# Four graph-attention layers on one core: the unmasked attention computed transposed, its denominators from column sums, and three kinds of elementwise work moved to ScalarE

## The reference

```python
out = relu(x @ mlp1_w + mlp1_b)                  # 512 features
residual = out
h = relu(out) @ W_fc                             # 512 x 512
e = leaky_relu(f1[:, None] + f2[None, :], 0.2)   # f1, f2: h times the halves of a_fc
att = softmax(e, axis=2)                         # over j, no mask
out = elu(elu(att @ h)) + residual
out = relu(out @ mlp2_w + mlp2_b)                # 256 features
...                                              # masked attention with W_hand, elu(elu(.)) + residual, relu
```

## Time and profile before

| quantity | value |
|---|---|
| median of 3 runs | 2882.01 us (2877.89 to 2885.95) |
| the profiled execution, its own time | 2880.97 us |
| span of its trace | 2879.2 us |
| mean granted TensorE clock | 0.996 of full speed |
| PE busy | 2827.2 us (98%) |
| DVE busy | 2551.1 us (89%) |
| ACT busy | 2169.4 us (75%) |
| POOL busy | 575.6 us (20%) |
| DMA over the span | 13 GB/s |

### The profile page before, as it was taken

The page is one execution under the profiler, slowest core; times in us unless marked ns, Lnnn a source line. Parts: engine busy times, 40 slices in busy tenths (PEclk is TensorE's granted clock), DMA queues, the critical chain, the costliest instruction groups (busy, mean ns, idle before and its releaser), DMA issues. The chain is left out here.

```text
span 2879.2 us, 66889 instructions
## 1 busy us (share of the span) xinstructions
PE 2827.2 (98%) x25368; PEld 2593.7 (90%) x25368; DVE 2551.1 (89%) x7305; ACT 2169.4 (75%) x5791; POOL 575.6 (20%) x731
## 2 busy tenths in 40 slices
PE   7999999999999999999999999999999999999998
PEld 7888998999999999998999999999989998999986
DVE  6898888998999899989988989889899888998977
ACT  5677778777777777787777787777777777777766
POOL 4021022211122211122211222111222111222001
PEclk8999999999999999999999999999999999999999
DMA  2000000000000000000000000000000000000000
GB/s 82 9 10 8 16 16 16 1 16 16 16 16 16 1 16 16 16 16 9 9 16 16 16 16 9 9 16 16 16 16 2 16 16 16 16 16 2 9 8 15
DMA packets 16800, 42.05 MB, mean 15 GB/s; under 512 B 5344, under 2 KB 7392, under 8 KB 16480
## 3 DMA queue, kind: packets, MB, share of 16 engines
q1 hardware_dynamic: 16480, 37.77, 3.7%
HBM read 20.99 MB, written 16.78 MB: 13 GB/s over the span
## 5 line engine op out<-in xcount | busy, mean ns | idle before, releaser
L690 PE MATMUL bank<-hw,R 128*128 128x257 f32 x3072 | 716.5, 381 | 4.4 <-DVE R L905 2.0
L690 PEld LDWEIGHTS bank<-hw,R 128*128 128x128 f32 x3072 | 562.2, 190 | 85.7 <-issue 11.1
L1380 POOL TENSOR_TENSOR rs<-ve,mhalf 128x4 f32<-128x4 f32 x128 | 133.5, 1043 | 1754.7 <-DVE ve L848 1649.5
L905 DVE SCALAR_TENSOR_TENSOR R<-bank,E,mask_ne 128x512 f32<-128x512 f32 x640 | 451.0, 741 | 19.1 <-PE bank L678 16.3
L592 PE MATMUL bank<-wfc_hi,oThi 128*128 128x256 f32 (+1 forms) x1024 | 302.5, 295 | 0.0
L592 PE MATMUL bank<-wfc_hi,oTlo 128*128 128x256 f32 (+1 forms) x1024 | 289.6, 283 | 0.0
L592 PE MATMUL bank<-wfc_lo,oThi 128*128 128x256 f32 (+1 forms) x1024 | 289.6, 283 | 0.0
L724 PEld LDWEIGHTS bank<-hw,R 128*64 128x64 f32 x8192 | 252.2, 139 | 29.3 <-issue 16.7
L724 PE MATMUL bank<-hw,R 128*64 128x65 f32 x8192 | 270.5, 225 | 6.6 <-DVE R L905 4.1
L1197 ACT ACTIVATE Z<-bank,rs 128x258 f32<-128x258 f32 (+1 forms) x384 | 177.8, 477 | 81.1 <-PE bank L592 80.8
L592 PEld LDWEIGHTS bank<-wfc_hi,oThi 128*128 128x128 f32 x1024 | 194.0, 189 | 1.7
(11 more groups left out here) (275 smaller groups left out, 8807.5 us busy)
## 6 DMA issues: line engine op xcount, KB each, us to landing
x<-in_x_dram SPq DMA_DIRECT2D x32, 512.0 KB, 3.5
out_dram<-x SPq DMA_DIRECT2D x31, 512.0 KB, 2.6
R<-in_adj_dram SPq DMA_DIRECT2D x2, 512.0 KB, 7.1
Z<-in_L_gnn_mlp_w_dram SPq DMA_DIRECT2D x2, 512.0 KB, 5.5
O<-in_L_gnn_W_fc_dram SPq DMA_DIRECT2D x1, 1024.0 KB, 6.8
out_dram<-x SPq DMA_DIRECT2D x4, 128.0 KB, 1.7
R<-in_L_gnn_W_dram SPq DMA_DIRECT2D x1, 256.0 KB, 3.8
R<-in_L_gnn_W_hand_dram SPq DMA_DIRECT2D x1, 256.0 KB, 6.6
```

Source lines behind the costliest of these rows:

```text
L690: ins = e.matmul(bk[:, 0:257], P[:, j, i * 128:(i + 1) * 128], hw[:, j, 0:257], start=(j == 0), stop=(j == NBLK - 1))
L905: e.scalar_tensor_tensor(P[:, t, :], bank_of(b, "row", p)[:, :], m["E"][:, 1, h, j:j + 1], mask[:, j, :], ALU.max, ALU.mult).then_inc(up(" ...
L1380: e.tensor_tensor(m["rs" + z][:, :], m["ve" + z][:, :], mhalf[:, :], ALU.pow).then_inc(up("rs", b), 1 if l == 1 else 3)
```

## The change

- **Inner attention.** Features are now the weights and P is streamed, 512 wide: four units `u` of 12 matmuls. The result is features x nodes at once, so the transposes `zT` are gone. `HA` loses its two extra columns.
- **Denominators.** POOL adds the four P blocks (`column_sums`: three additions of 128x512, a copy to hi, a subtraction for lo). PE sums over the partitions with 8 matmuls that stream two columns of ones, DVE takes the four reciprocals, PE spreads them over the partitions with 4 transposes, and ACT copies the row to `R[s][:, 3, :]`. DVE multiplies each unit by it (`scaled`).
- **The double elu.** ACT works on 512-wide tiles: relu of the negative, exp of its negative, second exp. DVE adds the residual to the relu part (`residual`) and joins (`joined`). The hi part goes to `Rr`, the lo part to `Zr`, so `oT` is free after `attf`, and ACT's next `m1` waits for `attf` of the batch before and no longer for its `m2`.
- **The order around P.** P is built before most of the lo parts of `HB`, and `USES` differs for lane 2.
- **Moved to ScalarE.** `center` of layers 2 and 3, and the minimum in layer 1's second attention (as relu of the negative and exp of its negative).
- `TURNS` is another table: `-        "w00ww0000ww0ww0000w00w11w0www0ww1111www1www00ww00w01...` becomes `+        "w00ww0000ww0ww0000ww0w011w0111101ww11wwwwwwww1001ww0...`, for every engine.

```diff
-        HA = {p: sb(f"HA{p}", [128, NBLK, F + 2], F32R) for p in PARTS2}
+        HA = {p: sb(f"HA{p}", [128, NBLK, F], F32R) for p in PARTS2}
...
-                    e.tensor_scalar(m["mn"][:, n:n + 1], m["sx"][:, n:n + 1], 1.0 / F, None, ALU.mult).then_inc(up("hn", b))
+                    e.activation(m["mn"][:, n:n + 1], m["sx"][:, n:n + 1], ACT.Copy, scale=-1.0 / F).then_inc(up("hn", b))
                     w.wait_ge(*at("hn", b, l - 2, n, 0))
-                    e.tensor_scalar(hns[s][:, n, :], x[:, n, :], m["mn"][:, n:n + 1], 0.0, ALU.subtract, ALU.max).then_inc(up("hn", b))
+                    e.activation(hns[s][:, n, :], x[:, n, :], ACT.Relu, bias=m["mn"][:, n:n + 1]).then_inc(up("hn", b))
...
-            for q in range(8):
-                i, H, n = q // 2, (HA, HB[s])[q % 2], 258 - q % 2 * 2
-                cols = slice(i * 128, (i + 1) * 128)
-                w.wait_ge(*freed(b, "attf", q))
+            def denominators():
+                w.wait_ge(*at("pq", b, 4))
+                w.wait_ge(*freed(b, "dn"))
+                bk = bank_of(b, "dn")
+                for i in range(NBLK):
+                    for k, c0 in enumerate((1536 + i * 128, i * 128)):
+                        ins = e.matmul(bk[:, 2 * i:2 * i + 2], Zr[s][:, c0:c0 + 128], ones[:, 0:2], start=k == 0, stop=k == 1)
+                ins.then_inc(up("dn", b))
+                yield
+                w.wait_ge(*at("rDf", b, 0))
+                for n in range(NBLK):
+                    ins = e.transpose(bk[:, n * 128:(n + 1) * 128], m["rD"][:, 0, n:n + 1].broadcast_to([128, 128]), ident[:, :])
+                ins.then_inc(up("dn", b))
+                yield
+
+            if len(RINGS[s]) == 2:
+                yield from denominators()
+            for u in range(4):
+                H, cols = (HA, HB[s])[u // 2], slice(u % 2 * 128, (u % 2 + 1) * 128)
+                w.wait_ge(*freed(b, "attf", u))
                 for j in range(NBLK):
                     w.wait_ge(*at("Plo", b, j))
-                    w.wait_ge(*at(("hAlo", "hBlo")[q % 2], b, j))
-                    ins = mm3(e, bank_of(b, "attf", q)[:, 0:n], (oT["hi"][:, j, cols], oT["lo"][:, j, cols]),
-                              (H["hi"][:, j, 0:n], H["lo"][:, j, 0:n]), j == 0, j == NBLK - 1)
-                    if j < NBLK - 1 and not i:
+                    w.wait_ge(*at(("hAlo", "hBlo")[u // 2], b, j))
+                    ins = mm3(e, bank_of(b, "attf", u)[:, :], (H["hi"][:, j, cols], H["lo"][:, j, cols]),
+                              (oT["hi"][:, j, :], oT["lo"][:, j, :]), j == 0, j == NBLK - 1)
+                    if j < NBLK - 1:
                         yield
                 ins.then_inc(up("attf", b))
                 yield
-            for fo in range(4):
-                w.wait_ge(*freed(b, "zT", fo))
-                bk = bank_of(b, "zT", fo)
-                c0 = (fo * 128 + 256) % 512
-                for n in range(NBLK):
-                    w.wait_ge(*at("zf", b, 7))
-                    i = e.transpose(bk[:, n * 128:(n + 1) * 128], Z[s][:, n * 512 + c0:n * 512 + c0 + 128], ident[:, :])
-                i.then_inc(up("zT", b))
-                yield
+                if u == 0 and len(RINGS[s]) > 2:
+                    yield from denominators()
...
+            def scaled(u):
+                w.wait_ge(*at("attf", b, u))
+                w.wait_ge(*at("rDr", b, 0))
+                e.tensor_tensor(Z[s][:, u * 512:(u + 1) * 512], bank_of(b, "attf", u)[:, :], R[s][:, 3, :],
+                                ALU.mult).then_inc(up("yf", b))
+                yield
...
+                e.scalar_tensor_tensor(y, y, 0.0, O1[:, (u + 2) % 4, :], ALU.max, ALU.add).then_inc(up("gf", b))
...
+                e.scalar_tensor_tensor(o, exf(u), -1.0, Z[s][:, u * 512:(u + 1) * 512], ALU.add, ALU.add).then_inc(up("o2", b))
...
+            w.wait_ge(*at("dn", b, 0))
+            e.reciprocal(m["rD"][:, 0, :], bank_of(b, "dn")[:, 0:8:2]).then_inc(up("rDf", b))
...
-                w.wait_ge(*at("m2", b - 1, 1))
+                w.wait_ge(*at("attf", b - 1, 3))
...
+                e.activation(exf(u), Z[s][:, u * 512:(u + 1) * 512], ACT.Relu, scale=-1.0).then_inc(up("ef", b))
+                w.wait_ge(*at("ef", b, u, 0))
+                e.activation(exf(u), exf(u), ACT.Exp, scale=-1.0).then_inc(up("ef", b))
...
+            def column_sums():
+                one, hi, lo = Z[s][:, 1024:1536], Zr[s][:, 1536:2048], Zr[s][:, 0:512]
+                for q in range(2):
+                    w.wait_ge(*at("P", b, 4, 2 * q + 1))
+                    if q == 0:
+                        w.wait_ge(*at("E", b, 1, 2))
+                    e.tensor_tensor(Z[s][:, q * 512:(q + 1) * 512], R[s][:, 2 * q, :], R[s][:, 2 * q + 1, :],
+                                    ALU.add).then_inc(up("pq", b))
+                    yield
+                w.wait_ge(*at("pq", b, 1))
+                e.tensor_tensor(one, Z[s][:, 0:512], Z[s][:, 512:1024], ALU.add).then_inc(up("pq", b))
```

More of the change, by code:

```diff
@@ L144 @@
[L144 to L147 removed]
+        "wwwww00wwww00w0000ww000000000w000000w1100000010010w000w01w0111w11111www10w011101100ww0w11010101001110111100000"
@@ L262, in build @@
         xs = [sb(f"x{i}", [128, NBLK, F]) for i in range(XSLOTS)]
-        R = [sb(f"R{s}", [128, PTILES, N]) for s in range(LANES)]
+        R, Rr = zip(*[sb2(f"R{s}", [128, PTILES, N]) for s in range(LANES)], strict=True)
         Z, Zr = zip(*[sb2(f"Z{s}", [128, 2080]) for s in range(LANES)], strict=True)
@@ L915, in divisor, with low_part @@
                 yield
-            def low_part(kind, name):
+            def low_part(kind, name, ns=range(NBLK)):
                 H = HA if kind == "hA" else HB[s]
-                for n in range(NBLK):
+                for n in ns:
                     w.wait_ge(*at(kind, b, n))
@@ new lines, in vector_batch @@
+            w.wait_ge(*at("dn", b, 0))
+            e.reciprocal(m["rD"][:, 0, :], bank_of(b, "dn")[:, 0:8:2]).then_inc(up("rDf", b))
+            yield
+            for u in range(4):
+                yield from scaled(u)
+                if u:
+                    yield from joined(u - 1)
+                yield from residual(u)
+                if u > 1:
+                    yield from low_o2(u - 2)
+            yield from joined(3)
+            yield from low_o2(2)
+            yield from low_o2(3)
@@ L1270, in scalar_batch, with high_hB @@
             yield
-            for n in range(NBLK):
+            def high_hB(n):
                 w.wait_ge(*at("hs2", b, n))
@@ L1274, in scalar_batch @@
                 yield
+            for n in range(3):
+                yield from high_hB(n)
             for j in range(NBLK):
+                if j == 1:
+                    yield from high_hB(3)
+                w.wait_ge(*at("hs2", b, 3))
                 w.wait_ge(*at("P", b, 4, j))
@@ L1300, in scalar_batch, with exf, elus @@
[L1300 to L1304 removed]
+            def exf(u):
+                return (R[s][:, 4, :], rowt[s][:, :])[u % 2]
+            def elus(u):
+                w.wait_ge(*at("yf", b, u))
+                if u > 1:
+                    w.wait_ge(*at("o2", b, u - 2))
+                e.activation(exf(u), Z[s][:, u * 512:(u + 1) * 512], ACT.Relu, scale=-1.0).then_inc(up("ef", b))
+                w.wait_ge(*at("ef", b, u, 0))
+                e.activation(exf(u), exf(u), ACT.Exp, scale=-1.0).then_inc(up("ef", b))
+                yield
@@ L1307, in scalar_batch @@
+            yield
+            for u in range(4):
+                yield from elus(u)
+                yield from again(u)
+                if u:
+                    yield from high_o2(u - 1)
+            yield from high_o2(3)
             for fo in range(2):
-                ta = ends[s][:, fo * 512:(fo + 1) * 512]
+                ta = Z[s][:, fo * 512:(fo + 1) * 512]
                 w.wait_ge(*at("m2", b, fo))
@@ L1356, in scalar_batch @@
                 yield
-            yield from squares(3, 2)
-            yield from squares(3, 3)
+            for i in (2, 3):
+                yield from center(e, w, b, 3, (i,))
+                yield from squares(3, i)
             yield from entry_sums(e, w, b + LANES)
@@ L1406, in pool_batch @@
             yield from power(e, w, b, 1)
+            yield from column_sums()
             yield from presum(2, 0)
```

412 lines of the change are left out of this document (196 added, 216 removed), and 4 rows, old and new, of the table ONCE.

## The result

| | median | runs | against before |
|---|---|---|---|
| before | 2879.97 us | 2877.89 to 2885.95 | |
| after | 2899.50 us | 2898.19 to 2901.52 | 1.0066 [1.0051, 1.0082] |

The account below looks back on a forecast made before the run. PE's solid row of matmuls was taken as the bound: 2880.97 us, less 29.8 for the shorter row, plus 3.2 for order and 2 for new waits, gives 2856.4, predicted as 2856 us; range 2836 to 2884.

Parts of the forecast that it names:

- PE's row: PE's sequence of matmuls and transposes: loses 13.20 us a batch, gains 12.27, so 0.93 shorter, 29.8 us over 32 batches.
- the borders: On PE, L592 matmuls behind four-head attention blocks: 62 instead of 30 of 128, costing 32 x 0.10 = 3.2 us.
- the lower bound of 0.057: Step in us between two-column matmuls at L767, from below; eight would take 0.46 us a batch, not 0.85.
- These edits cost nothing as long as PE's row covers them: Work added on DVE, ACT and POOL (213 us on POOL) stays hidden, since none reaches PE's 98% busy.
- POOL blocks DVE: Rival, 0.07: POOL operations hold up DVE's; one block of 1.13 us a batch reaching PE loses 36 us, 2892 us.
- The column sums come late: Rival, 0.07: POOL's sums delayed, PE stands at L767; 5.5 us behind loses 2.1 us a batch, 2923 us.
- The saved time turns into waits: Rival, 0.14, no change: ACT loses slack, its centring queues; 0.83 us more waiting a batch, 2873 to 2889 us.
- waits at L767 or L772: Sign of a wrong forecast: PE's waits for POOL at L767 or for `rD` at L772 reach tens of us.
- no 0.8 us a batch in the steady part: Sign of a wrong forecast: the span does not shorten by about 0.8 us for each steady-part batch.

Follow-up runs that it names:

- e5: Changed kernel without POOL's five column-sum steps; the small matmuls read block 0 of P, so denominators omit three quarters of the sum: 2859.99 us, 0.9931 of before.
- e9: Changed kernel with POOL's five column-sum steps kept but their results unread; the small matmuls read block 0 of P: 2896.77 us, 1.0057 of before.
- e6: Changed kernel with only the end of its order changed, batch 30 going through layers 2 and 3 beside batch 31: 2891.63 us, 1.0040 of before.
- e10: Changed kernel with three POOL steps, four small matmuls, and batch 30 beside batch 31 in layers 2 and 3: 2861.88 us, 0.9936 of before.
- e7: Changed kernel with denominators from four matmuls with ones as weights and a 512-wide DVE reciprocal, without POOL's steps: 2963.80 us, 1.0291 of before.
- e11: Changed kernel with three column-sum additions on DVE, four small matmuls, and batch 30 beside batch 31 in layers 2 and 3: 2884.60 us, 1.0016 of before.
- e4: Changed kernel with POOL making each of the two pair sums of P twice: 2942.78 us, 1.0216 of before.

## Why the prediction was wrong

- **PE's row was priced rightly.** e5 has all of the new row, small matmuls and spread included, and none of POOL's sums. For 21 batches it takes 2353.3 - 537.8 = 1815.5 us, 86.5 each, 0.9 less than before; 0.93 less was predicted (0.83 with the borders). In the kernel after, the eight two-column matmuls at 1391.0 us start 0.11 us apart (taken 0.106), and the lower bound of 0.057 is out. That e5's total of 2860 us lies so near 2856 is partly luck: against the kernel before, its profiled span is 18.1 us shorter up to batch 5, where five to six batches at 0.83 us would give about 5 (an estimate), 18.1 shorter between the marks, and 14.3 longer behind them, where about 4 were to be gained. What made the start shorter is not separated.
- **The failing step is "These edits cost nothing as long as PE's row covers them".** It was written with POOL's 213 us in it, as if an instruction on POOL took POOL's time alone. The five steps took DVE's too: 2491.8 - 2421.9 = 70 us, 2.2 a batch. By the means of the groups against e5, 41.5 us are in P's lo parts (1011 against 687 ns), 21.1 in P's blocks (705 against 540) and 9.5 in L893 (402 against 328); DVE's records overlap their neighbours a little, so these come to slightly more than 70. 36.8 / 32 = 1.15 us a batch reached the end, and the time came out slower where faster was forecast. The rival "POOL blocks DVE" had the mechanism and the rows; its chance of 0.07 was the mistake. That its price, one block of 1.13 us a batch (2892), is so near 1.15 is luck: waits of up to 1.3 us at L670 and L682, in some batches only, add up to it.
- **Why the chance was too low.** The argument against it was that `presum` blocks in the same way already and PE hardly waits. The new ones start when P is being made, and behind the held lo parts DVE's queue has `tm` and `A`, for which PE's whole row waits: 21.4 of the 23.5 us between the marks. That `presum` costs little because nothing urgent stands on DVE beside it is an argument; no run moved the sums to another place.
- By the rule of the Trainium skill ("SBUF — State Buffer", section on the two sides) that was quoted for it, e9 and e5 agree for the lo parts, which have two SBUF operands: 1011 ns with POOL's steps beside, 687 without. The blocks of P have one SBUF tensor and columns as scalars, which the rule as quoted does not name, and were held as well: up to 1522 ns in e9, at most 547 in e5.
- **"The column sums come late" was small**: at most some 3 us in all, by e9, and not clear of the noise. **"The saved time turns into waits" for lack of ACT** did not happen: ACT has the same 2282 us in e5, which took 2860. The sign that the prediction named for the lateness, waits at L767 or L772, did not appear; the other sign, no 0.8 us a batch in the steady part, did.
- **The end was not priced.** The prediction gave each batch the same gain and never looked at what the new table does when the batches run out. It is the second term that was put at nothing. e6 gets 7.9 us back by order alone. In the changed kernel 508.5 us lie behind the mark of batch 26, before 489.7: 18.8 more. It is 2857.3 - 2353.3 = 504.0 in e5, without holds, and 496.4 in e10. What keeps even e10 above before is not separated.

In one line: 2880.0 before, less 20.0 for everything but the sums (e5, 2860.0), plus 36.8 for POOL's working beside DVE (e9) and 2.7 for what is left, is 2899.5. The 20.0 already carries what the start gained and the end lost.

## What to carry to other kernels

Work that is moved to an idle GpSimd costs more than GpSimd's own time. Here five steps of 128x512 that read SBUF cost DVE 2.2 us a batch and the end 1.15. Price such work as DVE time too, and look at which DVE instructions stand beside and behind it and who waits for them. When a helper's cost is in doubt, keep its work and let nobody read it: that tells the cost of the work from the cost of the wait in one run. A table of order needs its last two batches looked at by themselves; fewer helper steps (three instead of five here, without the sum's lo part) and an interleaved end made the changed kernel the faster one by 0.6%, 2861.9 against 2880.5 us.

## What was not expected of the hardware

- DVE operations of one SBUF tensor and per-partition scalars are held too: 528/541/1522 ns (shortest, median, longest) for 128x512 in e9, 528/540/547 in e5, and for 128x4 (L893) a mean of 402 ns, 328 in e5.
- A reciprocal of 128x512 on DVE took 3351 ns in e7, 6.5 ns a column; one of 128x4 from the same kind of bank took 174 in the kernel after.
- A POOL addition of two SBUF tiles of 128x512 took 1375 ns (L1430), the same addition on DVE 685 ns in e11. The copy L1437 of the same width, with one operand, took 640 to 900 ns by its groups.
- Each extra POOL addition of e4 cost DVE half its own time: POOL's busy time rose by 88 us for 64 instructions, DVE's by 42 us.
